# Group loop of a Mamba-style layer: operands moved into accumulation banks, and the next group's convolution tiles spread over steps 4 to 7

## What is computed

```
proj = x @ in_proj_w.T              # gate, (x, B, C) = hbc, dt
xBC  = silu(conv4(hbc))             # causal, 4 taps per channel
dt   = softplus(dt + dt_bias);  dA = exp(-dt * exp(A_log))
state = state * dA + (dt * x) B^T   # per token, 64 heads of 64, 8 groups
y    = state C + x * D              # D: one skip factor per head
yn   = y * rsqrt(mean(y*y per group) + eps) * norm_weight * silu(gate)
out  = yn @ out_proj_w.T
```

## Time and profile before

| | us |
|---|---|
| median of 3 runs | 1824.86 (1823.95 to 1825.76) |
| profiled execution | 1824.79 |
| its span | 1823.0 |
| first transposes of group 0 to first transposes of the last group | 863.03 |
| the last group, to the transposes of the next stage | 130.99 |

### The profile page before, as it was taken

The page is one execution under the profiler, slowest core; times in us unless marked ns, Lnnn a source line. Parts: engine busy times, 40 slices in busy tenths (PEclk is TensorE's granted clock), DMA queues, the critical chain, the costliest instruction groups (busy, mean ns, idle before and its releaser), DMA issues.

```text
span 1823.0 us, 26503 instructions
## 1 busy us (share of the span) xinstructions
PE 1573.8 (86%) x8870; PEld 1231.1 (68%) x8870; DVE 1392.2 (76%) x2223; ACT 760.7 (42%) x1390; POOL 1026.2 (56%) x861
## 2 busy tenths in 40 slices
PE   3788999989989999899899869997589999988791
PEld 2577777767777777687677647885357676666581
DVE  5578998989989989989999875556537776768525
ACT  2344444434443434344344213332136766664131
POOL 3267777677678676866876864003433443327544
PEclk9899999999999999999999888998689999998696
DMA  3111011021021110110211021122000000041344
GB/s 112 35 36 63 19 47 58 12 69 35 12 74 35 46 58 17 66 37 12 75 35 33 27 64 58 69 69 92 1 1 13 1 13 1 1 160 72 104 139 161
DMA packets 49496, 92.59 MB, mean 51 GB/s; under 512 B 8016, under 2 KB 32720, under 8 KB 44176
## 3 DMA queue, kind: packets, MB, share of 16 engines
q1 hardware_dynamic: 45744, 79.58, 13.4%
q0 software_dynamic: 3680, 12.06, 2.0%
HBM read 81.14 MB, written 10.49 MB: 50 GB/s over the span
## 4 chain that ended last, share of the span: by engine, by line
PE 58%; DVE 25%; issue 7%; POOL 4%; ACT 4%; DMA 1%; SPq 0%; DVEq 0%; POOLq 0%; ACTq 0%
PE banks L350 31%; PE banks L1723 6%; DVE tap L1191 3%; PE banks L1842 3%; PE banks L1733 2%; PE banks L1801 2%; DVE y L1276 2%; PE banks L1832 2%; PE banks L1616 2%; DVE em L1306 2%; DVE wcl L355 2%; PE banks L1656 2%; DVE ynTl L355 1%; DVE acc L618 1%; PE banks L1647 1%
## 5 line engine op out<-in xcount | busy, mean ns | idle before, releaser
L1191 DVE SCALAR_TENSOR_TENSOR tap<-banks,parg,tap 128x511 f32<-128x511 f32 (+2 forms) x288 | 214.8, 746 | 23.9 <-ACT tap L918 17.1
L700 POOL TENSOR_TENSOR am<-ah,upto 128x1024 fp32r<-128x1024 f32 x64 | 129.6, 2026 | 161.1 <-PE banks L1616 121.4
L350 PE MATMUL banks<-xTh,wch 128*128 128x512 f32 x384 | 170.7, 444 | 23.0 <-DVE sg L1245 22.9
L853 POOL TENSOR_SCALAR kz<-kst,head 128x512 fp32r<-128x512 f32 x64 | 99.1, 1567 | 159.9 <-DVE kst L1420 159.9
L1306 DVE TENSOR_TENSOR em<-em,gmask 128x1024 f32<-128x1024 f32 x64 | 141.9, 2217 | 21.6 <-ACT em L970 21.1
L350 PE MATMUL banks<-xTh,wcl 128*128 128x512 f32 x384 | 155.4, 405 | 0.0
L350 PE MATMUL banks<-xTl,wch 128*128 128x512 f32 x384 | 155.0, 404 | 0.0
L926 ACT ACTIVATE th<-tap 128x512 f32<-128x512 f32 x96 | 60.8, 633 | 218.5 <-DVE tap L1191 215.6
L700 POOL TENSOR_TENSOR am<-al,upto 128x1024 fp32r<-128x1024 f32 x64 | 149.1, 2330 | 0.0
L1123 ACT ACTIVATE prob<-banks,nmax 128x128 f32<-128x128 f32 (+3 forms) x256 | 121.9, 530 | 54.3 <-DVE nmax L1436 54.1
L1436 DVE TENSOR_REDUCE nmax<-banks 128x2 f32<-128x256 f32 (+3 forms) x128 | 104.8, 819 | 39.8 <-PE banks L1833 39.7
(11 more groups left out here) (290 smaller groups left out, 4571.6 us busy)
## 6 DMA issues: line engine op xcount, KB each, us to landing
x<-grownT SPq DMA_DIRECT2D x96, 128.0 KB, 4.7
x<-in_w_conv SPq DMA_DIRECT2D x7, 1536.0 KB, 6.7
x<-in_w_gate SPq DMA_DIRECT2D x8, 1024.0 KB, 4.8
x<-in_w_out SPq DMA_DIRECT2D x8, 1024.0 KB, 4.8
eraw<-in_expert_w SPq DMA_DIRECT2D x8, 1024.0 KB, 7.7
gur<-in_ff_gu SPq DMA_DIRECT2D x7, 1024.0 KB, 4.7
x<-in_hidden SPq DMA_DIRECT2D x16, 256.0 KB, 3.8
mates<-yd SPq DMA_DIRECT2D x8, 512.0 KB, 4.3
```

What stands on the lines that cost most here:

```text
L350: m = nc.tensor.matmul(o, a, b, start=first and n == 0, stop=last and n == len(terms) - 1)
L700: m = pool.tensor_tensor(am[:, part, :, :], a[:, i, :].bitcast(F32).unsqueeze(2).to_broadcast([P, HG, P]), upto[:, :].unsqueeze(1).to_broa ...
L853: m = pool.tensor_scalar(kz[:, quad % 2, p2, j, :], kst[:, p2, :].bitcast(F32), head[:, j:j + 1], None, ALU.mult)
L1191: nc.vector.scalar_tensor_tensor(tap[:, q % 2, sh:L], bk(CONV_BANKS[q % 2])[:, 0:L - sh], parg[:, KC * q + k:KC * q + k + 1], tap[:, q % 2 ...
```

## The change

- Exp works in place: ScalarE writes it back into banks 2 and 3 (`decayed`), and VectorE multiplies it from there by gmask into em. TensorE waits for that multiply (m_ready) before it writes banks 2 and 3 again, where it waited for exp (e_ready).
- The skip term is made by ScalarE: four scaled copies of xbc into a new tile xd at the end of each step. VectorE adds bank 7 and y into bank 7, and then xd to it in one instruction.
- The gate multiply reads bank 7 and writes yn into bank 6; ScalarE and VectorE make ynTh and ynTl from there. TensorE writes bank 7 only after yn is made (yn_ready), and bank 6 only after ynTl.
- ysq now shares its memory with y.
- The residuals of the convolution weights are made in three couples of 256 columns (1024 elements): one by VectorE in step 3, one by GpSimd at the end of its step 3, one at the end of its step 4. ScalarE rounds all three after exp. TensorE waits for the couples one by one.
- The next group's six tiles are spread as 1, 2, 2, 1 over steps 4 to 7. A step with one tile uses bank 0 alone.
- The grownT store counts on small_in; later counts are one higher.

```diff
+        decayed = banks[:, 2:4, :].rearrange("p b (h t) -> p (b h) t", t=P)
+        def couple(t, n):
+            return t[:, :, 2 * n * P:2 * (n + 1) * P]
-            if s in (4, 5, 6) and not last:
-                return (NB * CT + 2 * (s - 4), NB * CT + 2 * (s - 4) + 1)
+            if s >= 4 and s < NT and not last:
+                return tuple(NB * CT + q for q in ((0,), (1, 2), (3, 4), (5,))[s - 4])
# sync engine
-                sp.wait_ge(wc_lo2, 2 * g + KT + 2)
+                sp.wait_ge(wc_lo2, g + 1)
# GpSimd, end of step
-                if s == 3 and not last:
-                    for k in (2, 3):
-                        pool.wait_ge(wc_hi, KT * g + KT + k + 1)
-                        low(pool, wcl[:, k, :], conv_stage(1)[:, k, :], wch[:, k, :]).then_inc(wc_lo, 1)
+                if s in (3, 4) and not last:
+                    pool.wait_ge(wc_hi, 3 * g + KT + s - 1)
+                    low(pool, couple(wcl, s - 2), couple(conv_stage(1), s - 2), couple(wch, s - 2)).then_inc(wc_lo, 1)
# ScalarE
-                    nc.scalar.copy(ynTh[:, :, :], y[:, :, :]).then_inc(ynT_hi, 1)
+                    nc.scalar.copy(ynTh[:, :, :], kt(bk(6))).then_inc(ynT_hi, 1)
-                    nc.scalar.activation(em[:, s % 2, :, :], banks[:, 2:4, :].rearrange("p b (h t) -> p (b h) t", t=P),
-                                         ACT.Exp).then_inc(e_ready, 1)
+                    nc.scalar.activation(decayed, decayed, ACT.Exp).then_inc(e_ready, 1)
+                    for n in range(CT // 2):
+                        nc.scalar.copy(couple(wch, n), couple(conv_stage(1), n)).then_inc(wc_hi, 1)
-                    nc.scalar.activation(ysq[:, :, :], y[:, :, :], ACT.Square).then_inc(sq_ready, 1)
+                    nc.scalar.activation(ysq[:, :, :], kt(bk(7)), ACT.Square).then_inc(sq_ready, 1)
+                if s < NT:
+                    if not (first and s == 0):
+                        act.wait_ge(y_ready, NT * g + s)
+                    for k in range(KT):
+                        n = nc.scalar.activation(xd[:, k, :], xbc[:, k, s * P:(s + 1) * P], ACT.Copy, scale=skipg[:, k:k + 1])
+                    n.then_inc(xd_ready, 1)
# VectorE
-                    low(nc.vector, ynTl[:, :, :], y[:, :, :], ynTh[:, :, :]).then_inc(ynT_lo, 1)
+                    low(nc.vector, ynTl[:, :, :], kt(bk(6)), ynTh[:, :, :]).then_inc(ynT_lo, 1)
-                    nc.vector.tensor_tensor(em[:, s % 2, :, :], em[:, s % 2, :, :],
+                    nc.vector.tensor_tensor(em[:, s % 2, :, :], decayed,
-                        nc.vector.tensor_tensor(y[:, :, :], y[:, :, :], kt(bk(7)), ALU.add).then_inc(y_part, 1)
+                        nc.vector.tensor_tensor(kt(bk(7)), kt(bk(7)), y[:, :, :], ALU.add).then_inc(y_part, 1)
-                        skipped(y)
-                    else:
-                        skipped(kt(bk(7)))
+                    dve.wait_ge(xd_ready, NT * g + i + 1)
+                    nc.vector.tensor_tensor(kt(bk(7)), kt(bk(7)), xd[:, :, :], ALU.add).then_inc(y_ready, 1)
-                    for k in (0, 1):
-                        dve.wait_ge(wc_hi, KT * g + KT + k + 1)
-                        low(nc.vector, wcl[:, k, :], conv_stage(1)[:, k, :], wch[:, k, :]).then_inc(wc_lo2, 1)
+                    dve.wait_ge(wc_hi, 3 * g + KT + 1)
+                    low(nc.vector, couple(wcl, 0), couple(conv_stage(1), 0), couple(wch, 0)).then_inc(wc_lo2, 1)
+                    if c < CH - 1:
+                        dve.wait_ge(state_ready, m + c + 1)
-                    nc.vector.tensor_tensor(y[:, :, :], y[:, :, :], gate_at(i % NT), ALU.mult).then_inc(yn_ready, 1)
+                    nc.vector.tensor_tensor(kt(bk(6)), kt(bk(7)), gate_at(i % NT), ALU.mult).then_inc(yn_ready, 1)
# TensorE
-                        pe.wait_ge(e_ready, NT * g + s)
+                        pe.wait_ge(m_ready, NT * g + s)
-                        pe.wait_ge(wc_lo, 2 * g + KT + 2)
-                        pe.wait_ge(wc_lo2, 2 * g + KT + 2)
+                        pe.wait_ge(wc_lo2, g + 1)
+                    elif s > 4:
+                        pe.wait_ge(wc_lo, 2 * g + KT + min(s - 4, 2))
+                    at_least(pe, ynT_lo, NT * g + i)
-                    if not (first and s == 1):
-                        pe.wait_ge(y_ready, NT * g + i)
+                    at_least(pe, yn_ready, NT * g + i)
-                if tiles:
-                    pe.wait_ge(e_ready, NT * g + s + 1)
+                if len(tiles) > 1:
+                    pe.wait_ge(m_ready, NT * g + s + 1)
```

More of the change, by code:

```diff
@@ L912, in _, with first_tap @@
             norm_scalar(0)
-            def first_tap(n, q):
+            def first_tap(n, q, bank):
                 act.wait_ge(h_ready, n + 1)
@@ L917, in first_tap @@
                     act.wait_ge(xbc_ready, n - 1)
-                nc.scalar.activation(tap[:, q % 2, :], bk(CONV_BANKS[q % 2]), ACT.Identity,
+                nc.scalar.activation(tap[:, q % 2, :], bk(bank), ACT.Identity,
                                      bias=parg[:, CT * KC + q:CT * KC + q + 1],
@@ L1190, in convolve @@
                         dve.wait_ge(taps, 3 * n + sh - 1)
-                    nc.vector.scalar_tensor_tensor(tap[:, q % 2, sh:L], bk(CONV_BANKS[q % 2])[:, 0:L - sh],
+                    nc.vector.scalar_tensor_tensor(tap[:, q % 2, sh:L], bk(bank)[:, 0:L - sh],
                                                    parg[:, KC * q + k:KC * q + k + 1],
@@ L1236, in _ @@
             decays_of(0)
-            convolve(1, 1)
+            convolve(1, 1, CONV_BANKS[1])
             silu(0, 0, 0)
@@ L1271, in entered_part @@
                         nc.vector.tensor_tensor(y[:, :, :], kt(bk(6)), grown, ALU.mult).then_inc(yo_used, 1)
-                def skipped(base):
-                    for k in range(KT):
-                        n = nc.vector.scalar_tensor_tensor(y[:, k, :], xbc[:, k, i % NT * P:(i % NT + 1) * P], skipg[:, k:k + 1],
-                                                           base[:, k, :], ALU.mult, ALU.add)
-                    n.then_inc(y_ready, 1)
                 if s == 4 and not last:
@@ L1310, in step @@
                 if tiles:
-                    convolve(n0 + tiles[0], tiles[0] % CT)
+                    convolve(n0 + tiles[0], tiles[0] % CT, CONV_BANKS[0])
+                if s == 0:
+                    nc.vector.tensor_copy(skipg[:, :], skip[:, bass.ds(g, 1), :].rearrange("p g k -> p (g k)"))
                 if making:
@@ L1577, in _, with convolved @@
             pe.wait_ge(wdt_lo, 1)
-            def convolved(n, q, b):
+            def convolved(n, q, b, bank):
                 ch, tok = slice(q * P, (q + 1) * P), slice(b * L, (b + 1) * L)
-                products(bk(CONV_BANKS[q % 2]), [(wch[:, k, ch], wcl[:, k, ch], xTh[:, k, tok], xTl[:, k, tok])
+                products(bk(bank), [(wch[:, k, ch], wcl[:, k, ch], xTh[:, k, tok], xTl[:, k, tok])
                                                  for k in range(KT)]).then_inc(h_ready, 1)
```

73 lines of the change are left out of this document (31 added, 42 removed).

## The result

The changed kernel takes 1804.91 us (1799.42 to 1805.99), the kernel before, run beside it, 1825.31: a ratio of 0.9883 [0.9862, 0.9904]. I had forecast 1783.0 in a range of 1757 to 1820. The sign is right and the time is in the range, though outside 1765 to 1803, the forecast's own step bounds. 20.4 us were saved and not 42: half. The profiled execution took 1805.31 us, 19.5 less than the one before.

A forecast was written before the change was run, and what follows sets the result against it. TensorE and VectorE pass the lead: VectorE is late in steps 2 to 4, TensorE sets the pace elsewhere. Seven groups saving 4.5 us each (31.5) plus 10 in the last make 41.5 us, so 1783 us, range 1757 to 1820.

The forecast's parts named there:

- Operands in banks: VectorE's em, ynTl, yn and skip term use accumulation banks: with the residuals 190 us less VectorE work, not itself the gain.
- (a): Scores of the next step and the second convolution tile wait for em's multiply instead of exp: no cost.
- (b): Output products into bank 7 wait for the gate multiply of the tile before: no cost.
- the second rival: Bank writes cost double, VectorE is late again and the gain is eaten: 1805 to 1835, about 1821 us; chance 0.14.
- Spread and couples, steps 4, 5, 7: Tiles moved, gate product waiting for taps in steps 4 and 7, late gate weights in 5: 14.4, 16.4, 14.5 us.
- Step 2: VectorE waits for GpSimd's state decay until 11.9 us; its later work slips 1.9 us, hidden; step 15.95 us.
- the 11.6 us of step 3: Wait for y gone, one new wait of 1.2 us for ynTl: 11.6 to 11.7 us (10.5 to 13.1).
- my own signs of being wrong: Bank-to-bank adds over 1 us, xtok waiting for xd, group-loop TensorE clock under 0.97, or step 3 above 13 us.
- The last group: Group without next tiles: step 3 saves 5.6 us, step 2 1.2, the six steps after 3 to 4; together 10.
- (c): Entering-state products wait for ynTl: nothing behind a convolution tile, 1.2 us in step 3 with nothing in front.
- The slower one: Waits in steps 4, 5 and 7 each pass 3.2 us and bring half clock: 1842 us; chance 0.10.
- The floor: The new waits of steps 3, 4, 5 and 7 don't form: 86 us saved, 1739 us; chance 0.10.

The follow-up runs named there:

- experiment 1: The changed kernel with the next group's six tiles back at 2, 2, 2, 0 over steps 4 to 7: 1790.75 us, ratio 0.9804.
- experiment 3: The changed kernel with the gate product of one-tile steps 4 and 7 in bank 2 instead of bank 0: 1817.68 us, ratio 0.9960.
- experiment 4: The changed kernel with both of GpSimd's couples of convolution residuals made in step 3: 1804.32 us, ratio 0.9889.
- experiment 9: The changed kernel with the last group's VectorE norm round in the middle of the next step, before em's multiply: 1802.48 us, ratio 0.9881.
- the corrected kernel: The changed kernel, spread kept, with gate product in bank 2, both couples in step 3, state decay first, last group's norm round mid-next-step: 1743.92 us.

## Why the prediction was half right

**Operands in banks, the waits (a), (b): right.** Each bank term came out within 0.03 us per instruction. The couple of residuals takes 2.44 us where I took 2.0, and VectorE is at 90.1 us per group against 88. The four xd copies took 1.27 us where I took 1.2. The reasoning that this is not the gain, since TensorE keeps all its products, held, and so did the fall of the second rival, writes into a bank at double cost: its 1805 to 1835 lies next to the measured time by chance. The Trainium skill's rule that a bank source is dearer on VectorE ("VectorE: DVE Perf Modes", the TRN2 errata section) had no effect that the trace shows: 676 ns at least for ynTl from a bank, 680 from the working memory.

**Spread and couples, steps 4, 5, 7: right.** Forecast 14.4, 16.4, 14.5; measured 14.48, 16.60, 14.47, by the waits and causes named (experiments 1, 3, 4). Steps 0, 1, 2, 6: 15.05, 14.9, 15.95, 15.95 against 15.08, 14.92, 15.90, 15.90. The gate weights' casts began 3.8 us into step 5, 3.4 said.

**Step 2 failed, and with it the 11.6 us of step 3.** I saw the state decay late behind the wol residuals, at 11.9 us (11.8 by my own terms; measured 11.77), let VectorE's later work slip by 1.9 us, and called that "still inside TensorE's 15.95". It isn't inside: silu, taps, tanh and xd are the queue in front of the next xtok and ynTh, so the slip arrives in step 3 as waits of 1.20 and 0.93 us. My own numbers said so: xd had "1 us of cover", and a slip of 1.9 us is more than that. I also gave silu no stretch; beside GpSimd it took 1.94 us and not 0.68, and I had left it out of the list of those that read two operands from SBUF. The tanh that I had over at 14.4 us began at 16.6. And in every second group the clock halves behind the two waits (14.62 against 12.97 us), while the same waits in the groups between bring nothing. Step 3 took 13.8 us on average, 2.2 over the forecast and above my upper bound of 13.1. Two of my own signs of being wrong came true: step 3 above 13 us, and xtok standing behind xd. The groups behind the first took (935.29 - 208.34)/6 = 121.2 us (the second's first transposes are at 208.34), 2.4 over the sum of 118.8, so this step is nearly all of it. Experiment 5 made the state decay first and got 11.15, with xd where it was.

**Seven equal groups: an error that hid part of the miss.** I multiplied one late group's 4.5 us by seven, but against 123.3, the mean that holds the shorter first group. That one went from 119.0 to 115.5; the other six went from 124.0 to 121.2. So the six were 14.2 us over my sums together, and the first was 3.4 under: luck, not foresight.

**The last group: forecast 10 us saved, measured 0.9 lost.** The term is "step 3 5.6, step 2 1.2, the six steps after it 3 to 4". The waits for y (3.29 us in step 3) went, and the five for GpSimd's sums (1.86, 2.55, 3.95, 0.91 and 2.12 us in TensorE's timeline of before, 11.4) shrank to 2.4. But I named the new wait (c), entering-state products for ynTl, with "ynTl ends at 2.5 to 4: nothing", from the loop's steps, and didn't look at what else VectorE has queued in this group. The last group's waits after the change, TensorE, and what VectorE does ahead of the longest:

```profile
986.62 1.72 PE L1636 MATMUL banks<-xbc,state 128*128 128x128 f32 x8 [1.97 <-DVE ynTl L360]
1000.22 1.16 PE L1636 MATMUL banks<-xbc,state 128*128 128x128 f32 x8 [1.47 <-DVE ynTl L360]
1013.53 1.23 PE L1642 MATMUL banks<-em,dtx 128*64 128x128 f32 x16 [3.60 <-DVE ynTl L360]
...
1027.55 2.08 PE L1636 MATMUL banks<-xbc,state 128*128 128x128 f32 x8 [5.19 <-DVE ynTl L360]
...
1039.95 1.16 PE L1636 MATMUL banks<-xbc,state 128*128 128x128 f32 x8 [1.75 <-DVE ynTl L360]
...
1050.05 2.08 PE L1636 MATMUL banks<-xbc,state 128*128 128x128 f32 x8 [2.26 <-DVE ynTl L360]
```
```profile
1022.09 1.98 DVE L623 TENSOR_SCALAR acc<-acc,mv,rs 128x512 f32<-128x512 f32 x1
1023.99 2.11 DVE L628 TENSOR_SCALAR acc<-x,mv,rs 128x512 f32<-128x512 f32 x1
...
1026.81 0.68 DVE L360 TENSOR_TENSOR ynTl<-banks,ynTh 128x512 fp32r<-128x512 f32 x1
```

Six waits, 16.2 us, behind a norm round that before the change held up output products alone. The first of them is only in part the norm round's: it lies in step 3, where step 2's slip arrives here too (a wait of 1.84 us for the state, a silu of 1.86), and the state decay first took 3.9 us off that step. Experiment 9 moved the norm round and got 14.5 back. So 10.9 us of the miss are here and 31.5 - 20.6 = 10.9 in the loop: together the 21.9 by which 1804.9 stands over 1783, but for 0.1.

**The rivals.** The slower one's condition (a wait from 3.2 us on) was set too high: waits of 1.20 and 0.93 us close together, or one of 2.08, were followed by half clock in some groups and not in others. In the change it stayed at about one stretch per two groups, so its price of 1842 wasn't reached. The floor, 1739 by my working, is near where the corrected kernel arrived (1743.9), though that is another kernel, and its last group gave more (15.2 us, 12 said) and its loop less (66.1, 73.5 said): the waits that I put against it are real, and four small edits remove most of them.

## What to carry to other kernels

When an instruction slips, follow its queue into the next step before calling it hidden: the test is not whether TensorE is still busy, but whether anything at the start of the next step stands behind it. A new wait is to be priced in each form of the loop, the written-out last group above all, where another stage's work stands in the same queue. Where the pacing engine has several waits of 1 to 3 us, one fix at a time may show nothing or a loss (0.6 us and -12.8 us in experiments 4 and 3), and all together 61 us; judge each by its step in the trace, not by the total, and look whether the steps that the edit doesn't touch stayed as they were.

## What the runs showed of the hardware

- Half clock moves. The change has it in step 3 of every second group; with those waits removed it was in step 4 of some groups instead (16.04 us at 0.89, experiment 5; in experiment 4, which leaves step 3 alone, it is in step 4 of just the groups that don't have it in step 3), behind a wait of 2.1 us that does not bring it in the change. With nearly all waits gone the granted clock of the loop is 1.00 (0.99 in the change, 0.98 before).
- The same silu beside the same GpSimd instructions, issued at the same distance (0.10 and 0.11 us behind am's start), took 2.3 us or 4.4: who gets the port pair between two GpSimd instructions isn't fixed. On each em or ynTl with a bank operand, beside the same GpSimd work, the spread was 11 and 17 ns over 64 executions.
- A VectorE addition within one bank takes 0.69 us for 512 elements, as a multiply from a bank into SBUF does; an exp of 1024 elements back into its two banks takes 1.01 us on ScalarE, 1.02 into SBUF in the kernel before.
